# Two float32r parts instead of three bf16 parts for queries and keys, the conv stacks written in place, two heads in the two halves of the partition rows

## The reference, cut to what matters

```python
# first layer, per batch
q = einsum('bcn,dc->bnd', xf, wq) + bq          # 16 channels
k = einsum('bcn,dc->bdn', xf, wk) + bk[:, None]
attn = softmax(einsum('bnd,bdm->bnm', q, k))    # 1024 x 1024
x = x + einsum('bcj,bij->bci', v, attn)
# then t = x as tokens; a = layernorm(t)
q, k, v = split(a @ in_w.T + in_b)              # global: 8 heads of 16 channels
attn = softmax(q @ k.T / 4)                     # 8 heads x 1024 x 1024
# a second, local attention (window 5, 4 heads), a fusion network, a feed-forward network,
# two layer norms; t += that; then a mixture of 8 experts of 1280 places each; t += that
```

## Time and profile before

| | |
|---|---|
| median of 3 runs | 1704.99 us (1702.29 to 1707.94) |
| the profiled execution's own time | 1713.91 us |
| its span | 1711.8 us |
| mean granted TensorE clock | 0.947 |
| busy: TensorE, VectorE, ScalarE, GpSimd | 1547.5, 1369.4, 1023.9, 628.9 us |

### The profile page before, as it was taken

One profiled execution on the slowest core, in us unless ns is written; L12 is line 12 of the kernel. 1 busy time (PEld: TensorE's weight loads), 2 busy tenths in 40 slices (PEclk: granted clock), 3 DMA queues, 4 the chain that ended last, 5 costly groups with the idle time before them and its releaser, 6 DMA issues.

```text
span 1711.8 us, 24948 instructions
## 1 busy us (share of the span) xinstructions
PE 1547.5 (90%) x8470; PEld 759.4 (44%) x8470; DVE 1369.4 (80%) x2806; ACT 1023.9 (60%) x1947; POOL 628.9 (37%) x1027
## 2 busy tenths in 40 slices
PE   4858899999999999999998999999989998879993
PEld 1523433443444345434543364425433433349992
DVE  4169798789988998998888988998789883747984
ACT  1411566576767676867675768676666677415443
POOL 4112210104532444245224352454245455324562
PEclk8776899999999999999999999999999998989997
DMA  3165642053305321542045113621262111033335
GB/s 81 51 169 185 205 123 77 27 138 95 114 18 154 101 97 37 156 130 81 27 124 155 44 61 107 164 73 30 73 179 85 54 69 43 10 82 107 111 119 212
DMA packets 126988, 169.89 MB, mean 99 GB/s; under 512 B 16144, under 2 KB 88773, under 8 KB 126862
## 3 DMA queue, kind: packets, MB, share of 16 engines
q1 hardware_dynamic: 117742, 157.44, 31.0%
q0 software_dynamic: 4608, 7.30, 1.3%
q10 hardware_dynamic: 4512, 3.56, 0.7%
HBM read 107.17 MB, written 62.52 MB: 99 GB/s over the span
## 4 chain that ended last, share of the span: by engine, by line
PE 57%; DVE 18%; ACT 8%; DMA 5%; POOL 5%; issue 4%; SPq 2%; ACTq 1%; POOLq 0%; DVEq 0%
PE bank L1621 9%; PE bank L1590 8%; PE bank L1609 8%; PE bank L1545 7%; DVE gmax L2242 5%; PE bank L1855 4%; DVE cmax L2181 3%; PE bank L1464 3%; ACT prob L1991 2%; PE bank L1658 2%; PE bank L1537 2%; PE bank L1648 2%; DMA gparts_d<-parts 2%; PE bank L1559 2%; DMA kv_d<-lqkv 2%
## 5 line engine op out<-in xcount | busy, mean ns | idle before, releaser
L1991 ACT ACTIVATE prob<-bank 128x512 f32<-128x512 f32 x1024 | 572.3, 595 | 281.9 <-PE bank L1609 279.3
L2242 DVE TENSOR_REDUCE gmax<-bank 128x1 f32<-128x512 f32 x1024 | 656.1, 681 | 45.4 <-PE bank L1590 43.8
L1590 PE MATMUL bank<-k_stack,q_stack 96*128 96x512 bf16 x1024 | 400.8, 397 | 36.1 <-DVE gmax L2242 19.1
L1609 PE MATMUL bank<-q_stack,k_stack 99*128 99x512 bf16 x1024 | 388.1, 387 | 25.5 <-ACT prob L1991 17.9
L1621 PE MATMUL bank<-prob,v_tok 128*32 128x512 f32 x2048 | 280.2, 621 | 0.0
L1378 POOL TENSOR_TENSOR lprod<-ql_tok,kv_win 128x640 f32<-128x640 f32 x64 | 100.5, 1591 | 359.4 <-DMA ql_tok<-ql_d 344.1
L1590 PEld LDWEIGHTS bank<-k_stack,q_stack 96*128 96x128 bf16 x1024 | 100.5, 99 | 276.4 <-DVE gmax L2242 171.8
L1609 PEld LDWEIGHTS bank<-q_stack,k_stack 99*128 99x128 bf16 x1024 | 99.8, 99 | 187.1 <-ACT prob L1991 131.3
L1385 POOL TENSOR_TENSOR lprod<-ls,kv_win 128x640 f32<-128x640 f32 x64 | 81.7, 1298 | 264.8 <-DVE ls L2298 264.8
L1545 PEld LDWEIGHTS bank<-cv_tok,cprob 128*128 128x128 f32 x960 | 117.6, 197 | 27.0 <-DVE t_tok L2209 14.4
L1545 PE MATMUL bank<-cv_tok,cprob 128*128 128x129 f32 x960 | 125.2, 284 | 2.3 <-ACT cprob L1939 1.4
(11 more groups left out here) (291 smaller groups left out, 2471.4 us busy)
## 6 DMA issues: line engine op xcount, KB each, us to landing
kv_win<-kv_d SPq DMA_DIRECT2D x32, 1280.0 KB, 5.7
kv_d<-lqkv SPq DMA_DIRECT2D x64, 128.0 KB, 2.2
gparts_d<-cprob SPq DMA_DIRECT2D x24, 256.0 KB
gparts_d<-parts SPq DMA_DIRECT2D x24, 256.0 KB
q_stack<-gparts_d SPq DMA_DIRECT2D x32, 192.0 KB, 3.1
k_stack<-gparts_d SPq DMA_DIRECT2D x16, 384.0 KB, 5.5
rows_d<-rows SPq DMA_DIRECT2D x10, 528.0 KB, 6.0
cprob<-rows_d SPq DMA_DIRECT2D x8, 660.0 KB, 5.6
```

What stands on the lines that cost most here:

```text
L1590: mm(max_ps[max_bank(n)][:, :], q_stack[quad][0:KROWS, h, i * P:(i + 1) * P], key_slot(b, quad)[0:KROWS, h, j * HN:(j + 1) * HN], start=Tr ...
L1609: mm(score_ps[n % 2][:, :], key_slot(b, quad)[0:KM, h, j * P:(j + 1) * P], q_stack[quad][0:KM, h, half * HN:(half + 1) * HN], start=True, ...
L1991: nc.scalar.activation(prob[:, g % 2, h, :], score_ps[n % 2][:, :], ACT.Exp).then_inc(exp_made, 1)
L2242: v.tensor_reduce(gmax[:, h, i, j:j + 1], max_ps[max_bank(n)][:, :], AX.X, ALU.max)\
```

## The change

- `KROWS` goes from 96 to 48 (three products of parts: high x high, high x low, low x high) and `KM` from 99 to 50 (two rows for the maximum). Parts are float32r, two of them. The stacks of a pair of heads lie one at rows 0 to 49, the other at rows 64 to 113 (`Z` = 64, `rows_of`). Each product reads one half of the rows.
- `max_at` makes consecutive `max_tile` steps alternate between the halves, consecutive `score_tile` steps do so by head, `conv_max` by key half; `conv_exp` uses the low half for four steps, then the high half. Every such product is still a step of its own (`PAIRS` is defined and not used).
- First layer: `conv_q` (two steps) and `conv_k` (one) replace `conv_qk`, `split`, `split_low0`, `conv_stacks`. The weights `cqw`, `ckw` hold the 16 channels three times, so the product itself lays out the stack, in two products per step with 64 output rows each. ScalarE writes the whole stack from PSUM, then VectorE overwrites the rows of the low parts (two instructions of 32 or 16 rows per step). No DMA.
- Global heads: ScalarE writes the high part once, VectorE the remainder from PSUM (`remainder`), once per 512 columns. `store_parts` (two DMAs of float32) replaces three of bf16; `stack_runs` issues four DMAs instead of three. The scale 0.25 goes into the weight.
- The negative maxima: three VectorE instructions instead of five, two DMAs instead of three.
- Four more small loads of biases at the start, two memsets, `k_stack`'s rows of ones set in six memsets of 32 rows.
- The planner: new durations, `SHIFTS` is emptied, a PSUM bank that two engines read in turn is held until the last, and each engine takes a step once.

```diff
-KROWS = TERMS * D
-KM = KROWS + 3
+Z = P // 2
+KROWS = 3 * D
+KM = KROWS + 2
+RUNS = [(0, 0, 1), (1, 0, 2)], [(0, 0, 2), (2, 0, 1)]
-NEG_STEPS = 5
+NEG_STEPS = 3
+PAIRS = TILES // 2
...
 SHIFTS = [
-    ("conv_qk", 1, -12.0), ("local_qkv", 0, -3.0), ...   # 35 entries, all removed
 ]
...
+        s.add("head", a, ("conv_q", h), (a, ("load_x",)), (a - 1, ("conv_exp", 1, NT - 1)), banks=ps)
+    s.add("head", a, ("conv_k",), (a, ("load_x",)), banks=ps)
...
 def max_at(n):
-            return m // NT, HT * half + m % NT // 2, m % 2
+            return m % 2, m // NT // 2, HT * half + m // 4 % HT, m // 2 % 2
...
+            def store_parts(b, w):
+                for h in range(2):
+                    head_done(sp, b, ("global_qk", w - 1, h))
+                for s in range(2):
+                    sp.dma_start(gparts_d[b, w - 1, :, s], split_home(b, w)[s]).then_inc(gsplit_out[w - 1], 16)
...
+            def conv_q(b, h):                                   # TensorE
+                ps, full = head_fill(pe, b, ("conv_q", h))
+                for z in range(2):
+                    last = mm(ps[rows_of(z, Z), :], cqw[:, :], x_cm[:, h * HN:(h + 1) * HN], start=True, stop=True)
+                last.then_inc(full, 1)
...
             def max_tile(b, quad, n):                           # TensorE
-                mm(max_ps[max_bank(n)][:, :], q_stack[quad][0:KROWS, h, i * P:(i + 1) * P],
-                   key_slot(b, quad)[0:KROWS, h, j * HN:(j + 1) * HN], start=True, stop=True).then_inc(max_full, 1)
+                z, w, i, j = max_at(n)
+                mm(max_ps[max_bank(n)][:, :], q_stack[quad][rows_of(z), w, i * P:(i + 1) * P],
+                   key_slot(b, quad)[rows_of(z), w, j * HN:(j + 1) * HN], start=True, stop=True).then_inc(max_full, 1)
...
+            def conv_q(b, h):                                   # ScalarE
+                ps, _ = head_read(act, b, ("conv_q", h))
+                if b:
+                    head_filled(act, b - 1, ("conv_exp", 1, NT - 1))
+                to(cq_stack[:, h * HN:(h + 1) * HN], ps[:, :], bias=cols[:, COL["cq"]:COL["cq"] + 1]).then_inc(chi_made, 1)
...
+            def remainder(dst, ps, bias, part):                 # VectorE
+                return v.scalar_tensor_tensor(dst, ps, bias, part, ALU.add, ALU.subtract)
+            def global_qk(b, w, h):
+                ps, free = head_read(dve, b, ("global_qk", w, h))
+                dve.wait_ge(ghi_made, 4 * b + 2 * w + h + 1)
+                hi, lo = split_home(b, 1 + w)
+                remainder(lo[:, n].bitcast(F32R), ps[:, :], bias, hi[:, n]).then_inc(free, 1)
```

More of the change, by code:

```diff
@@ L196 @@
 }
+READ_BY_ALL = {"conv_q", "conv_k", "global_qk"}
 BESIDES = {"pe": 0.0, "act": 0.0, "dve": 0.0, "pool": 0.0, "sp": 0.0}
@@ L326, in plan @@
                 if engine == "pe":
-                    part_of[n, "read"] = len(parts) + (1 if k + 1 < len(PARTS[step[0]]) else 0)
+                    last = len(PARTS[step[0]]) - 1
+                    part_of[n, "read"] = len(parts) + (last - k if step[0] in READ_BY_ALL else min(1, last - k))
                 part_of[n, "end"] = len(parts)
@@ L371, in plan @@
             free[engine] = starts[k] + time
-            orders.setdefault(engine, []).append(step)
+            if step not in begun.setdefault(engine, set()):
+                orders.setdefault(engine, []).append(step)
+                begun[engine].add(step)
         return orders
@@ L377 @@
 TAIL_PS, MAX_PS, SCORE_PS = ("tail", 1), ("max", 3), ("score", 2)
-def split_of(s, a, w, low, after):
-    s.add("split", a, ("split", w), (a, after))
-    s.add("split", a, low, (a, ("split", w)))
+WEIGHT_PS = ("weight", 3)
 def head_a(s, a, ps=HEAD_PS):
     for h in range(2):
[L389 to L392, removed]
+        s.add("head", a, ("conv_q", h), (a, ("load_x",)), (a - 1, ("conv_exp", 1, NT - 1)), banks=ps)
+    s.add("head", a, ("conv_k",), (a, ("load_x",)), banks=ps)
     for h in range(2):
@@ L399, in head_a @@
     for t in range(2 * NT):
-        s.add("head", a, ("conv_max", t), (a, ("conv_stacks",)), banks=ps)
+        s.add("head", a, ("conv_max", t), (a, ("conv_k",)), (a, ("conv_q", 1)), banks=ps)
     s.add("head", a, ("conv_guard",), (a, ("conv_max", 2 * NT - 1)), banks=ps)
@@ L598, in all_steps @@
     for i in range(FIRST_WEIGHTS, WEIGHTS):
[L599 removed]
+        s.add("x", 0, ("weight", i), (0, ("weights",)), banks=WEIGHT_PS)
     s.add("x", 0, ("fold",), (0, ("weight", WEIGHTS - 1)))
@@ new lines, in conv_k @@
+            def conv_k(b):
+                ps, _ = head_read(act, b, ("conv_k",))
+                if b:
+                    head_filled(act, b - 1, ("conv_exp", 1, NT - 1))
+                to(ck_stack[:, :], ps[:, :], bias=cols[:, COL["ck"]:COL["ck"] + 1]).then_inc(chi_made, 1)
+            def global_qk(b, w, h):
+                ps, _ = head_read(act, b, ("global_qk", w, h))
+                if h == 0 and w == 1:
+                    after(act, gsplit_out[1], b * 32)
+                bias = hcols[:, 0:1] if w == 0 else cols[:, COL["gk"]:COL["gk"] + 1]
+                to(split_home(b, 1 + w)[0][:, h * HN:(h + 1) * HN].bitcast(F32R), ps[:, :], bias=bias).then_inc(ghi_made, 1)
```

337 lines of the change are left out of this document (147 added, 190 removed).

## The result

| | before | after |
|---|---|---|
| median in the same call | 1706.2 us | 1908.7 us |
| span of the profiled execution | 1711.8 us | 1906.7 us |
| mean granted TensorE clock | 0.947 | 0.858 |

The ratio is 1.120, 95% interval 1.116 to 1.124: slower by 202 us by the medians, 205 by the ratio of the runs. The forecast was 1692 us with a range of 1636 to 1742, so the time lies far outside, beyond the slow rival.

What follows compares the result with a forecast made beforehand. TensorE and VectorE, coupled by PSUM banks, were taken to pace the kernel together. Start -20, TensorE 0, VectorE -7, added waits +4 and order +10 gave -13 us on 1705, so 1692 us, range 1636 to 1742.

Steps and rivals of the forecast that it cites:

- Start: Start of the kernel: three gains from earlier first-layer and key-stack work, together -20 us, bounds -8 and -26.
- first piece: First-layer stacks at the start: without the stack DMA the first conv_max comes 5 to 10 us sooner, 8 taken.
- The second: Key parts after batch 0's last projection: two instructions replace three split steps, so their store starts sooner; 4 us taken.
- third piece: conv_max of batch 1 fills the engines' 12.28 us idle hole before the key stack; 8 us taken.
- (a): TensorE in the middle: two heads' products in different row halves overlap, 81 to 92 pairs, -19 us a batch.
- (c): TensorE in the middle: float32r products start 0.23 us apart against 0.22, weight load not counted; +3 us a batch.
- (b): TensorE in the middle: 48 round trips a batch between half-row and full-array products at 0.3 us, +14.4 us a batch.
- rule of exchange: Middle batches: a microsecond of work on TensorE or VectorE moves a batch by half a microsecond, the other staying put.
- VectorE, -7 us: VectorE in the middle: fewer subtractions and guard steps against added remainders, net -1.9 us a batch, half felt over seven.
- R2: Slow rival: shape changes cost 0.42 us with exposed loads, only 50 pairs form; about 1740 us, chance 0.25.
- R1: Fast rival: halves overlap and row changes are cheap, so VectorE becomes the bound; 1636 us, chance 0.2.
- R3: Rival: halves do not overlap at all and nothing drains, +6 us a batch on TensorE; 1720 us, chance 0.15.

Runs made afterwards that it cites:

- e3: Changed kernel with every stack product reading all 128 rows (full array) instead of one half, float32r kept; 1765.3 us, ratio 1.034 to the kernel before.
- e6: Kernel before, its global max_tile and score_tile products reading only rows 0 to 65 of the bf16 stacks; 1742.7 us, ratio 1.023.
- e4: Changed kernel with every stack product reading rows 0 to 65, full-array in shape; 1841.2 us, ratio 1.079 to the kernel before.
- m1: Blocks of 60 bf16 or float32r products on 128, 96, 48 or alternating 48 rows, plus alternating shapes, behind the changed kernel's end; alternating pairs every 0.216 us (bf16).
- e5: Changed kernel with every stack product reading the low half only, so no pairs; 2067.5 us, ratio 1.213 to the kernel before.
- e2: Kernel before, its global max_tile and score_tile products reading only rows 0 to 63 of the bf16 stacks; 1825.1 us, ratio 1.073.
- e7: Changed kernel with stack products on all 128 rows and the global stacks read as bf16; 1750.3 us, ratio 1.024 to the kernel before.
- e1: Kernel before with its list SHIFTS emptied, nothing else; 1726.2 us, ratio 1.011.
- m2: Blocks of products on 66 to 128 rows, and 32-column float32 products followed by stack-like ones, behind the changed kernel; float32r blocks 0.227 us per product.
- e8: Changed kernel, halves kept, its global max_tile and score_tile products reading the stacks as bf16; 1851.6 us, ratio 1.085 to the kernel before.

## Why the prediction was wrong, by its own steps

**Start, forecast -20 us.** The first piece was right: six products ran side by side, and `conv_max` came 6.9 us sooner (forecast 5 to 10). They took 4.2 us and not 5.4 since the clock rose among them, which is luck. The second was right at its place and lost behind it. The store of the key parts is issued at 87.36 us, 4.4 sooner than in the earlier trace rows (forecast 4), but the load of the key stack is not. SyncE's queue after, and then before:

```profile
80.97 2.64 SPq L1120 DMA_DIRECT2D t_old<-kept_d  x1
83.65 1.66 SPq L1121 DMA_DIRECT2D a_old<-kept_d  x1
85.41 1.92 SPq L1127 DMA_DIRECT2D gparts_d<-parts  x1
87.36 0.75 SPq L1127 DMA_DIRECT2D gparts_d<-split_x  x1
...
99.15 1.73 SPq L1145 DMA_DIRECT2D k_stack<-gparts_d  x4
```

```profile
99.87 1.79 SPq L1177 DMA_DIRECT2D k_stack<-gparts_d  x3
```

From the end of the store's issue to the load it is 11.0 us after, and 6.2 us before. In the 11 us lie the flight of 1.0 MB of parts and two loads of 512 KB: these, `t_old` and `a_old`, now stand ahead of that store in the queue. That they cause the longer flight was not tried. The third piece, `conv_max` of batch 1 in the hole, failed: they start at 126.06 us (122.89 in the earlier trace rows), and the hole grew to 15.55 us. At 100 to 150 us the clock is 0.50, at 150 to 200 us 0.65, where before it was 0.57 and 0.78. With that the start turned into a loss of 13 us at the first score, against a forecast gain of 20. In e3, whose start differs in the rows of the stack products, that loss is 2 us, with clocks of 0.65 and 0.80.

**The clock was not among the terms at all, and this is the step that failed.** The earlier trace rows had 0.99 in the middle and 0.57 early; I took the first as given for the changed kernel too, and the second as a matter of idle time only. The middle (150 to 1340 us) ran at 0.87 and not 0.98, and the whole had 542 us at 1.2 GHz instead of 181. At the price above this is an estimated 126 us of the 195 between the two profiled executions. The clock was lower where the stack products used fewer rows, with TensorE busy 90 to 93%: 36 us (before to e6) to 76 us (e3 to e4), with no change of shape in either. In the changed kernel 2048 + 256 products use 48 or 50 rows, and in 200 us 123 of 212 slots hold one product alone. m1 has the same two cases by themselves: one half alone at 0.50, alternating halves at 0.99.

**(a) Pairs, -19 us a batch, and (c) float32r, +3: the count right, the first slot of a run mis-sized.** In 200 us, one batch, 89 pairs start within 0.03 us of each other: 62 of different lines, 27 inside one line. The forecast was 81 to 92. Against e5 they bring 23 us of time a batch, some 16 of it beside the clock. But every slot was taken as one product's 0.23 us; the first of a run is 0.34, single or pair, since the next load starts 0.11 us late and takes 0.19. This belongs to term (c), and not to the pairs: the argument from the earlier trace rows that loads do not count was drawn from an unbroken row. In this kernel the stack products come in ones to fours between others. Over the whole kernel the format costs 16 us in the full array, where (c) came to +10, and 59 in the halves, of which some 17 are clock.

**(b) Change of shape, 0.3 us: 0.19 to 0.30 for bf16 (e2, m1), 0.39 for float32r (m1), against bounds of 0.24 to 0.42.** The count of 48 a batch also held: 46 changes into full-array products and 52 back, in 200 us. With 0.39 the term is +19 us a batch instead of +14.

**(a) and (b) together, -5 us a batch, nearly held at the full clock.** There the changed kernel and its full-array twin e3 start 5.11 and 5.13 products per microsecond, so pairs and changes of shape cancel; as (b) and the first slots were dearer than forecast, that they come out even is in part luck. The kernel before starts 5.31; what lies between it and e3 is order, format and the open part below.

**The rule of exchange, half a microsecond per microsecond, is neither confirmed nor refuted.** e2 against e6 has 12 to 17 us more of TensorE's time a batch and is 10 to 12 us a batch longer; less the clock it is 9 to 11, so from a half to nine tenths is felt. e3 against e7 has 0.10 us more in each of some 480 first slots, 48 us, and is 16 to 18 us longer: a third is felt.

**VectorE, -7 us:** its busy time rose by 7 us over the eight batches, where -1.9 a batch was forecast. The three-operand remainder takes 0.742 to 0.751 us, for 16, 32 and 128 rows alike, where 0.685 was taken, and there are 10 a batch. Both are small beside the idle time.

**Order, +10 us:** 19 (e1).

**The sum in the runs' terms,** each the difference of two measured ratios (rounded), and beside it how the time at 1.2 GHz changed:

| step | us | at 1.2 GHz, us |
|---|---|---|
| order without shifts (e1) | +19 | +23 |
| the rest on the full array, read as bf16 (e1 to e7) | +22 | -40 |
| float32r in the full array (e7 to e3) | +16 | +2 |
| fewer rows at work (e3 to e4) | +76 | +193 |
| change of shape, one half alone (e4 to e5) | +229 | +310 |
| pairs (e5 to after) | -159 | -127 |
| together | +205 | +361 |

The 22 us of the second line stay open. The added waits of VectorE for ScalarE, the key stores' flight and an order planned with other durations are candidates; none was tried alone. Open too is why 66 rows cost clock inside the kernels (0.902 against 0.953) but not in the unbroken blocks of m2, and whether the changes of shape lower the clock by themselves: from e4 to e5 they came in together with 48 and 50 rows.

R2 had the right direction and nearly the right price (0.42 us, measured 0.39), but not the cause: it said 1740 and left the clock out. R1's observation, that halves overlap, was right too, and did not save it. R3 is refuted by equal starts.

## What to carry to other kernels

Half the rows is half the work only in an unbroken run of pairs. Here pairs among full-array products did no better at the full clock than the same products on the full array, because the change of shape each way and the exposed weight load at the start of each run took back what they saved; and the clock then fell. Before a layout with fewer rows, count the changes of shape and the starts of runs, price each, and ask first what the clock does: a mean clock read from the kernel before is no property of the kernel after. The shortest test is one line: read the old operands over 64 and over 66 rows. It separates the change of shape from the fewer rows, once the clocks of both are compared. To split a loss after the fact, count products per microsecond at each level of the clock.

## What the runs showed of the hardware that was not expected

- TensorE busy without a gap on 48 rows of one half: the granted clock goes from 1.00 in the block before to 0.50. The same instructions in alternating halves bring it back to 0.99 (m1).
- A microsecond at 1.2 GHz costs this kernel 0.35 to 0.39 us (e3 to e4, and the counts in the changed kernel).
- 64 and 66 rows differ by 4 to 5% of this kernel's time (e2, e6).
- A float32r load of 0.2 us shows up once behind each change to other products: 0.12 us (m2), 0.34 instead of 0.24 us for the first slot, pair or single (after and e8, e3 and e7). In an unbroken row it does not: 0.233 us a pair, with two loads side by side (m1).
- 16, 32 and 128 rows cost VectorE the same 0.74 to 0.75 us for 512 columns in the three-operand form with PSUM and SBUF.
